# Building attention's one-hot of nodes with four scalar comparisons instead of one broadcast comparison, and setting attention's constants on VectorE instead of GpSimd

## What is computed

```
score = sum(K[src] * Q[dst], axis=-1) / sqrt(16)
score = exp(clip(score, -5, 5))
wV = segment_sum(V[src] * score[..., None], dst)
z = segment_sum(score, dst)
attn = wV / (z + 0.001)
h = layer_norm(x + attn, gamma1, beta1)
h = h + relu(layer_norm(h, gamma2, beta2) @ Wo + bo)
```

## Time and profile before

| | |
|---|---|
| time, median of 3 runs | 2209.89 us (2209.18 to 2212.15) |
| the profiled execution | 2211.75 us |
| its span, first to last instruction | 2210.0 us |
| GpSimd busy | 1210.7 us (55%) |
| VectorE busy | 1430.3 us (65%) |
| TensorE busy | 1544.4 us (70%) |
| ScalarE busy | 1073.4 us (49%) |

### The profile page before, as it was taken

How to read it: one execution, slowest core, us unless ns; L and a number is a source line. 1 busy time by engine, 2 the same in 40 slices (tenths; PEclk the granted TensorE clock), 3 DMA queues, 4 the chain that set the end, 5 groups by cost and what they waited for, 6 DMA issues and landing times. The chain is left out here.

```text
span 2210.0 us, 42037 instructions
## 1 busy us (share of the span) xinstructions
PE 1544.4 (70%) x7805; PEld 1039.9 (47%) x7805; DVE 1430.3 (65%) x3765; ACT 1073.4 (49%) x2519; POOL 1210.7 (55%) x1484
## 2 busy tenths in 40 slices
PE   2777776899999999999945455554555545555554
PEld 1222223465555666666634444544444445444453
DVE  8999996545656633335655666666666666666665
ACT  6788885434553422222234555455545545555442
POOL 6544444323544411111147777777777777777774
PEclk8555557999999999999965555555555565555555
DMA  4000001101111111102354444444444444444442
GB/s 146 0 0 0 0 0 46 47 28 45 53 49 54 55 35 30 32 28 75 104 169 122 143 139 139 123 140 141 141 132 128 139 140 132 128 141 139 140 123 62
DMA packets 161687, 192.75 MB, mean 87 GB/s; under 512 B 42581, under 2 KB 129750, under 8 KB 161366
## 3 DMA queue, kind: packets, MB, share of 16 engines
q0 software_dynamic: 38784, 105.96, 16.3%
q1 hardware_dynamic: 122838, 86.10, 12.5%
HBM read 163.23 MB, written 25.04 MB: 85 GB/s over the span
## 5 line engine op out<-in xcount | busy, mean ns | idle before, releaser
L1479 POOL DMA_INDIRECT counts<-keys_values,a_index x788 | 782.5, 993 | 240.1 <-issue 194.7
L1590 PE MATMUL acc_bank<-counts 128*128 128x136 f32 x1616 | 422.5, 440 | 480.1 <-DVE counts L1710 456.0
L895 PE MATMUL z_bank<-y_parts,counts 128*128 128x384 bf16 (+1 forms) x3658 | 640.4, 327 | 1.2 <-DVE y_parts L1231 0.6
L1590 PEld LDWEIGHTS acc_bank<-counts 128*128 128x128 f32 x1616 | 360.6, 318 | 530.2 <-DVE counts L1710 500.1
L895 PEld LDWEIGHTS z_bank<-y_parts,counts 128*128 (+1 forms) x3658 | 357.8, 98 | 227.9 <-issue 4.1
L1699 DVE TENSOR_TENSOR counts<-aq_bank,counts 128x512 f32<-128x512 f32 x202 | 139.6, 691 | 343.3 <-DMA counts<-keys_values,a_index 256.2
L1536 ACT ACTIVATE counts<-a_clipped 128x32 f32<-128x32 f32 x202 | 46.3, 229 | 513.8 <-DVE a_clipped L1715 512.5
L428 POOL TENSOR_TENSOR key_low_build<-iota_b_build,src_cols_build 128x768 bf16<-128x768 bf16 x102 | 155.6, 1526 | 158.8 <-DVE flat_build L506 144.3
L1122 DVE TENSOR_REDUCE z_sum<-z_bank 128x128 f32<-128x384 f32 x150 | 83.6, 557 | 163.9 <-PE z_bank L895 159.6
L524 DVE TENSOR_TENSOR counts<-share_build,counts 128x300 f32 x408 | 166.7, 464 | 6.7 <-PE share_build L602 5.1
L602 PE MATMUL share_build<-flat_build,src_tile_build 128*128 128x300 bf16 x408 | 116.8, 443 | 71.6 <-ACT src_tile_build L568 42.8
(11 more groups left out here) (180 smaller groups left out, 2111.4 us busy)
## 6 DMA issues: line engine op xcount, KB each, us to landing
counts<-group_rel_rows SPq DMA_DIRECT2D x34, 768.0 KB
counts<-keys_values,a_index POOLq DMA_INDIRECT x788
self_term<-s_out SPq DMA_DIRECT2D x150, 64.0 KB, 1.6
s_in<-self_term SPq DMA_DIRECT2D x150, 64.0 KB, 1.8
counts<-query_parts SPq DMA_DIRECT2D x306, 10.5 KB
residual<-x_in SPq DMA_DIRECT2D x75, 64.0 KB, 1.6
counts<-counts SPq DMA_DIRECT2D x2, 1792.0 KB, 11.7
x_in<-in_x SPq DMA_DIRECT2D x50, 64.0 KB, 1.8
```

Of the source, the lines that this page charges most:

```text
L895: return nc.tensor.matmul(bank(p, dt)[:, 0:width], counts[:, bass.ds(dt.value(P) + source * NA, P)], y3[(p - 1) % 2][:, source, 0:width], ...
L1479: nc.gpsimd.indirect_dma_start(rows_kv[:, j, c, :], None, v.kv, bass.IndirectOffsetOnAxis(column, 0)).then_inc(gathered[j], 16)
L1590: ins = nc.tensor.matmul(acc_bank[ga.slot()][:, 0:TW], pick[:, s2.slot(MR), c, :], msg[:, s2.slot(MR), c, :], start=j == 2 and c == 0, sto ...
```

## The change

`pick` was made by one tensor_tensor over 4 x 128 x 128 elements, in which both operands are broadcast views in SBUF. It is now made by four tensor_scalar instructions of 128 x 128, one for each chunk: `iota` is the only tensor operand, and a column of `rel_cols`, one number for each partition, is the scalar. The last of the four signals `pick_done`. The six memsets move from GpSimd to VectorE; `iota` gets a semaphore of its own, and the waits are counted anew.

```diff
@@ attention
+        iota_ready = sem("a_iota")
...
         def _(pool):
-            nc.gpsimd.iota(iota[:, :].bitcast(I32), [[1, P]], base=0, channel_multiplier=0).then_inc(consts, 1)
-            pool.wait_ge(consts, 1)
-            nc.gpsimd.tensor_copy(iota[:, :], iota[:, :].bitcast(I32)).then_inc(consts, 1)
-            nc.gpsimd.memset(total[:, 1, :], 0.0).then_inc(consts, 1)
-            nc.gpsimd.memset(ones_row[:, :], 1.0).then_inc(consts, 1)
-            nc.gpsimd.memset(eps[:, :], EPS_LN).then_inc(consts, 1)
-            nc.gpsimd.memset(one[:, :], 1.0).then_inc(consts, 1)
-
-            nc.gpsimd.memset(five[:, :], 5.0).then_inc(consts, 1)
-            nc.gpsimd.memset(thousandth[:, :], 0.001).then_inc(consts, 1)
+            nc.gpsimd.iota(iota[:, :].bitcast(I32), [[1, P]], base=0, channel_multiplier=0).then_inc(iota_ready, 1)
+            pool.wait_ge(iota_ready, 1)
+            nc.gpsimd.tensor_copy(iota[:, :], iota[:, :].bitcast(I32)).then_inc(iota_ready, 1)
...
         def _(pe):
-            pe.wait_ge(consts, 5)
+            pe.wait_ge(consts, 6)
...
         def _(dve):
             chain = Chain(dve, dve_steps)
+            nc.vector.memset(total[:, 1, :], 0.0).then_inc(consts, 1)
+            nc.vector.memset(ones_row[:, :], 1.0).then_inc(consts, 1)
+            nc.vector.memset(eps[:, :], EPS_LN).then_inc(consts, 1)
+            nc.vector.memset(one[:, :], 1.0).then_inc(consts, 1)
+
+            nc.vector.memset(five[:, :], 5.0).then_inc(consts, 1)
+            nc.vector.memset(thousandth[:, :], 0.001).then_inc(consts, 1)
             dve.wait_ge(cols_ld, 32)
-            dve.wait_ge(consts, 8)
+            dve.wait_ge(consts, 6)
+            dve.wait_ge(iota_ready, 2)
...
                     (s - (MR - 1)).count(dve, agg_done)
-                    nc.vector.tensor_tensor(pick[:, s.slot(MR), :, :], rel_cols[:, bass.ds(s.value(GC), GC)].unsqueeze(2).to_broadcast([P, GC, P]),
-                                            iota[:, :].unsqueeze(1).to_broadcast([P, GC, P]), ALU.is_equal).then_inc(pick_done, 1)
+                    for c in range(GC):
+                        ins = nc.vector.tensor_scalar(pick[:, s.slot(MR), c, :], iota[:, :], rel_cols[:, bass.ds(s.value(GC) + c, 1)], None,
+                                                      ALU.is_equal)
+                    ins.then_inc(pick_done, 1)
```

## The result

The median of four runs is 2231.83 us (2227.25 to 2235.88) against 2210.67 for the kernel before (2209.18 to 2212.15): a ratio of 1.0087, 95% interval 1.0076 to 1.0099. The profiled execution took 2230.91 us with a span of 2229.1. 2185 was forecast, and the sign was wrong.

The account below looks back on a forecast made before the run. GpSimd's back-to-back gathers bound the kernel; of 37.0 us surplus 11.4 would remain, a gain of 25.6, or 25.3 with the last step, taking the median from 2209.89 to 2185 us; 8-in-10 range 2172 to 2232.

Parts of the forecast that it names:

- What bounds the kernel: GpSimd's gathers in attention: issued back to back at 1.25 us, plus 37.0 us surplus from those begun inside the old comparison.
- The comparison as GpSimd sees it: Gathers begun inside the four comparisons: each slips into a gap, losing 0.08 us instead of 0.26; gain 25.6 us.
- No other wait is next: GpSimd's waits after the gain: ring six deep, product asked for about two steps (10 us) later, so nothing is added.
- The 0.28 us on VectorE: Four comparisons take 0.88 instead of 0.60 a step, 57 us in all, covered by idle time; only 0.3 us paid.
- The constants: Six memsets moved at the start: GpSimd 0.4 us earlier, absorbed by a longer wait; worth 0.0, at most 0.4 either way.
- No hold at all: At the comparison: one tensor operand leaves GpSimd alone, the whole surplus goes, 2173.2 us; chance 0.10.
- The slower rival: At the comparisons: gathers are held while writing too, +23 us (2233) or +37 us (2247); chance 0.25.
- the likeliest case: Gathers slip in between the four comparisons: 2185 us, own range 2178 to 2196, chance 0.53.
- Third rival: VectorE's comparisons are held by gathers, 1.4 us more a step, so the gain goes: 2205 to 2214 us; chance 0.12.
- The rule of the Trainium skill: VectorE beside GpSimd: two-port instructions lock GpSimd out and starve descriptor writing; two-SBUF-input tensor_tensor hinders only reads. Spoke against the gain.

Follow-up runs that it names:

- the reduction in the middle: Kernel before plus an unused 0.28 us VectorE reduction in each step between comparison and scores: 2242.2 us, ratio 1.0128.
- reduction at the end: Kernel before plus the same unused 0.28 us VectorE reduction in each step, behind the clipping: 2211.2 us, ratio 0.998 against the kernel before.
- one-operand product: Changed kernel, message product replaced by a one-SBUF-operand reduction without score weighting: 2181.8 us, ratio 0.9857 to the kernel before; slower in three earlier runs (1.0099 to 1.0175).
- new order: Changed kernel with the four comparisons moved behind the clipping: 2188.6 us, ratio 0.9888 to the kernel before; slower in three earlier runs (1.0083 to 1.0139).

## Why the prediction was wrong

- **What bounds the kernel** was right: gathers at 1.25 us each from a start fixed by the first product, plus their surplus. In every profiled run where before took 2210 to 2214 us, the last gather's start is the thirteenth's plus 795 times 1.246 us plus the surplus, to within 4 us, and the span ends 28 to 29 us later.
- **The comparison as GpSimd sees it** was right for the gather it spoke of. I forecast 0.08 us for a third gather and comparisons of 0.30 at a pitch of 0.22. The median comparison is 0.28 at a pitch of 0.19, four take 0.86 to their recorded end, and 123 third gathers began among them, at the median 0.31 after the first as forecast, and lost 2.8 us, 0.02 each. None lost over 0.07, so none waited for the fourth comparison; I read that as a gather getting in between them.
- **The step that failed** is the sentence "No other wait is next": the sum put a new hold of the fourth gather at nothing. I looked for the next semaphore, not for the next instruction with the property that I had just named. L1710, 0.6 us behind the scores, has two SBUF tensors; a gather comes every 1.25 us; and the hold that I removed from the third gather was what kept the fourth 0.02 to 0.06 us clear of it. Shifting both through the rows of the kernel before would have given it: the message product began 1.19 after the comparison; with the 0.28 that I had forecast it holds from 1.47 to 2.06, and a fourth gather at 0.31 + 0.08 + 1.25 = 1.64 loses 0.42 us. In fact the message product moved by 0.18 and the third gather lost 0.02, which makes 1.96 - 1.58 = 0.38; the 121 fourth gathers that began inside the message product lost 0.37 at the median and 45.2 us together. This term is missing in the forecast's sum. The 0.28 us on VectorE, which I called covered since VectorE was idle a third of the time, was no cost in busy time but a shift in phase, and the reduction in the middle, which moves the message product by 0.27, prices that at 28 us.
- **The constants**: right, 0.0 within the interval. From the start of `iota` to the first gather 0.90 us pass instead of 1.22, and the thirteenth gather still waits for the first product. But it did not stay near 1150.6: attention itself began 1.7 us later. Below is the start of `iota` before, then both ends in the changed kernel.

```profile
1132.92 0.24 POOL L1460 IOTA a_iota<- 128x128 int32 x1 [8.36 <-POOLq L1259]
```

```profile
1134.66 0.24 POOL L1461 IOTA a_iota<- 128x128 int32 x1 [8.37 <-POOLq L1259]
...
1152.24 0.94 POOL L1472 DMA_INDIRECT counts<-keys_values,first_index  x1 [1.69 <-DVE counts L1700]
```

  That is no effect of the constants: in the profiled runs where before took 2210 to 2214 us, with them on GpSimd the thirteenth gather began at 1150.2 (reduction at the end) to 1153.7 us (in the middle), with them on VectorE at 1150.4 (one-operand product) to 1152.5 (new order).
- **The rivals.** No hold at all: no, but the loss at the comparisons is nearly nil. The slower rival gave 2233 us, close to the 2231.8, for a reason that the runs exclude: the held gather is the next one, by another instruction. My range reached up to 2232 because of that rival alone, so that the measured time lies just inside it is luck. (The upper end of the likeliest case, 2196, comes out of its own terms as 2195.) Third rival: single comparisons did wait, at most 0.52 us long (see the last section), but no four took over 1.06 together, where 0.9 + 4 x 0.27 was feared.
- **The rule of the Trainium skill** (SBUF — State Buffer, "Who interferes with whom"), as I weighed it, misled me. Its half on reads, that a VectorE instruction with two SBUF inputs contends with a GpSimd one that reads SBUF, fits nearly the whole of the loss (47.4 us inside the message product). Its half on two-port instructions, which made me give the slower case 0.25, would bear on 3.5 us at most here, those lost at the comparisons; and that the comparisons ran in such a mode is not shown: at 0.28 us they are no faster than L1634, a tensor_tensor of the same size.

## What to carry to other kernels

When two engines run in a fixed rhythm, an instruction's place against the other engine's is part of its price: list every instruction that can collide, and move all of them through the rhythm after the change, also when busy shares leave room. A delay that you remove may be what keeps the next event clear. A dummy instruction in two places of the same loop separates load from phase in two runs.

## What the runs showed of the hardware

A gather also holds VectorE, near its end. In the changed kernel, at the start of attention, a tensor_scalar of 34 elements took 0.40 us instead of the 0.24 of the earlier trace rows:

```profile
1140.85 0.94 POOL L1472 DMA_INDIRECT counts<-keys_values,first_index  x1 [0.30 <-issue]
...
1141.40 0.40 DVE L1631 TENSOR_SCALAR a_shift_col<-a_shift_col,lane_f 128x34 f32<-128x34 f32 x1
```

It began 0.55 into the gather and ended with it, at 1141.8; in the kernel before it had run from 0.14 to 0.38 of a gather, unhindered. The four comparisons take 0.86 together, but 1.00 to 1.06 in six steps: in four of them a gather began 0.01 to 0.06 us after the first comparison and ended shortly before the last did, in two it had begun 0.49 before and ended inside the four. Of the single comparisons 42 took over 0.40. I read it as the gather's writes near its end, which no run shows apart; these gathers themselves lasted no longer.

What holds a gather for long is an instruction with two tensors in SBUF, and not VectorE at work as such. Inside the products L1699 of the kernel before, one operand of which lies in PSUM, 51 gathers began while no other VectorE instruction ran, and lost nothing; inside L1700 of the changed kernel 65, with the same outcome.
